# Moving the depthwise convolution of a Mamba block from VectorE to TensorE, and two of GpSimd's B x products per batch element to VectorE

## The chip, the cores and the metric

One core of one Trainium2 chip runs the whole program in one launch. The metric is the device time of the launch in microseconds. The engines are called by the profile's names: PE (TensorE), DVE (VectorE), ACT (ScalarE), POOL (GpSimd) and SP (SyncE, which only issues DMAs here).

## The reference, cut to what matters

```python
x = L0_attn_x                                   # 8 x 512 x 256, float32
x = x + layernorm(mamba(layernorm(x)))
x = x + layernorm(moe(layernorm(x)))            # 8 experts, top 1, and a shared one

def mamba(x):                                   # D_INNER 512, D_STATE 16, D_CONV 4
    h = (layernorm(x) * norm_w + norm_b) @ in_proj_w.T
    hp = pad(h, 3 rows in front)
    h = silu(sum(hp[:, k:k + L] * conv_w[:, k] for k in range(4)))
    dt_in, B, C = split(h @ x_proj_w.T, [1, 16, 16])
    dt = softplus(dt_in @ dt_proj_w.T + dt_proj_b)
    for t in range(L):                          # for each channel and each of 16 states n
        state = exp(A * dt[t]) * state + B[t] * h[t]
        y[t] = sum over n of state * C[t] + D * h[t]
    return silu(y) @ out_proj_w.T + x
```

The change concerns the sum over the four taps (`conv_w`) and the product `B[t] * h[t]`. Both exist once per batch element, and there are 8 batch elements of 512 time steps.

## The kernel before, in words

Channels lie on partitions: the 512 inner channels are four chunks `c` of 128, and a chunk's 512 time steps lie along the free dimension. One batch element is one iteration `i` of the outer loop. Inside it a step number `q` runs from 0 to 31: `q = 16 h + n` is state `n` for the two chunks of half `h`, so every instruction of a step works on 128x1024 values.

A step is a pipeline over four engines:

- ACT makes the decay `exp(A dt)` in PSUM, two activations per step (`decays`, L702). There are two decay buffers, so the decay of step q+2 waits for the scan of step q.
- `bx = B x` has a ring of four buffers. For even q POOL makes it (`inject`, L484), out of rows of B that a DMA has spread over all partitions (`bbc`). For odd q DVE makes it (`inject`, L1040), out of a PSUM bank `psB` that PE fills with a broadcast row (`spread_b`, L1403). `psB` is one bank, so the next broadcast waits for the last DVE product.
- DVE runs the recurrence with one scan instruction per step (`scan`, L1052), on a ring of eight state buffers.
- POOL multiplies the state by C (`weigh`, L495), and PE adds it up in PSUM (`total`, L1411, three steps behind).

All engines work through a program order that is written out by hand. In step q of iteration i each engine does its part of the scan of batch element i, then `front(i + 1, q)`, the projections of the next batch element, then `back(i - 1, q)`, the output projection and norms of the one before. Every engine takes its instructions in this order and waits on semaphores.

The convolution belongs to `front`. For chunk c, at the even step 2c+2, PE multiplies by `in_proj_w` into the PSUM bank `psF` (L1330), and ACT copies it to `acc` times the last tap (L613). At the odd step 2c+3 DVE adds the three shifted taps out of `psF` with three `scalar_tensor_tensor` (L998). PE's next in-projection waits for that, since `psF` is one bank. At step 10 ACT loads the table for silu and makes `xh` (L619), silu of y of the batch element before (L669), and loads the exp table again. At 11 PE makes `dt_in` (L1337), at 14 the B and C rows (L1343), which ACT copies (`prow_kept`). PE's output projection of the batch element before follows at 15 and 17 (L1373), and DVE adds its result (L1021) at 16 and 18. At 20 POOL subtracts for softplus (L500), at 22 DVE adds the residual (L1028), and at 23 and 24 DVE takes a minimum (L1012).

In the last iteration (batch element 7) there is no `front`. In the first there is no `back`. After the last batch element comes the mixture of experts, which the change does not touch.

```python
                if q in (2, 4, 6, 8):                       # ACT, front
                    act.wait_ge(inproj_ready, C * f + c + 1)
                    nc.scalar.activation(acc[:, c], psF[:], ACT.Identity, scale=cw[:, c, TAPS - 1:TAPS])
                if q in (3, 5, 7, 9):                       # DVE, front
                    for m in range(1, TAPS):
                        last = nc.vector.scalar_tensor_tensor(out=acc[:, c, m:L], in0=psF[:, 0:L - m], ...)
```

## Time and profile before

| | us |
|---|---|
| median of three runs | 1540.49 |
| lowest and highest run | 1537.66, 1542.84 |
| the profiled execution | 1531.43 |
| its span, first to last instruction | 1529.5 |
| busy in the span: PE, DVE, ACT, POOL | 1191.8, 1042.3, 802.7, 1022.1 |
| mean granted TensorE clock | 0.903 of full speed |

The profile is one execution. The eight iterations over the batch elements lie between about 45 and 1017 us of the span, and the experts behind them. Times of rows are microseconds from the span's start. An engine's idle time before a row is given with what ended it.

### The profile page before, as it was taken

What the parts mean: (1) busy time and instruction counts of PE and PEld (TensorE: products, weight loads), DVE (VectorE), ACT (ScalarE), POOL (GpSimd) and SP (SyncE); (2) the same over time, 40 slices, a digit from 0 to 9 for tenths busy, and PEclk for the clock granted to TensorE, in tenths of its full rate; (3) what the DMA queues carried; (4) which work ended last, traced back from release to release, by engine and by line L of the source; (5) the groups of instructions that cost most, each with busy time, mean ns of one, the idle gap of its engine ahead of it and who ended that gap; (6) DMA issues with size and microseconds to landing.
All of it is one profiled execution on the core that took longest, in us unless ns stands there. A gap on an engine that the chain in (4) does not pass through costs nothing. (4 is left out here: it accounts for less than half of the span.)

```text
span 1529.5 us, 15586 instructions
## 1 busy us (share of the span) xinstructions
PE 1191.8 (78%) x4766; PEld 525.4 (34%) x4767; DVE 1042.3 (68%) x1051; ACT 802.7 (52%) x1386; POOL 1022.1 (67%) x476
## 2 busy tenths in 40 slices
PE   5775867878878867787788786665999989999940
PEld 2321213323323223232232221223466656566520
DVE  4698998998998978998999998853211123233237
ACT  6665667768758657677677655353111111111137
POOL 0599999999999999999999999950470000000025
PEclk9896999999989889899898898877999999999975
DMA  2802302401311220240230240024941021111135
GB/s 60 313 0 70 125 0 71 147 19 57 127 53 57 90 91 2 97 138 2 96 125 2 69 152 1 14 96 157 343 157 38 0 86 43 46 41 42 44 110 178
DMA packets 77953, 128.46 MB, mean 84 GB/s; under 512 B 7616, under 2 KB 56384, under 8 KB 73792
## 3 DMA queue, kind: packets, MB, share of 16 engines
q1 hardware_dynamic: 67120, 108.93, 21.0%
q10 hardware_dynamic: 7696, 10.36, 1.9%
q0 software_dynamic: 3072, 8.39, 1.7%
q8 instruction: 30, 0.49, 0.1%
q14 instruction: 35, 0.29, 0.1%
HBM read 95.94 MB, written 31.72 MB: 83 GB/s over the span
## 5 line engine op out<-in xcount | busy, mean ns | idle before, releaser
L495 POOL TENSOR_TENSOR state<-state,cbc 128x1024 f32<-128x1024 f32 x256 | 611.6, 2410 | 11.5 <-DVE state L1052 11.4
L1052 DVE TENSOR_TENSOR_SCAN state<-psX,bx 128x1024 f32<-128x1024 f32 x256 | 577.9, 2278 | 44.4 <-ACT psX L702 19.6
L702 ACT ACTIVATE psX<-dt,aneg 128x511 f32<-128x511 f32 x512 | 330.7, 679 | 222.4 <-DVE state L1052 220.7
L484 POOL TENSOR_TENSOR bx<-xh,bbc 128x1024 f32<-128x1024 f32 x128 | 309.3, 2417 | 63.4 <-DMA bbc<-bc_rows 42.8
L1411 PE MATMUL psY<-state,ident 64*64 64x512 f32 x2048 | 302.5, 684 | 59.9 <-POOL state L495 59.9
L561 POOL DMA_INDIRECT fy<-slot_out,slot x32 | 33.2, 1037 | 339.8 <-DMA slot_out<-yo 330.4
L1403 PE MATMUL bank<-prow,ident 128*128 128x512 f32 x256 | 151.8, 677 | 105.0 <-DVE bx L1040 104.9
L1040 DVE TENSOR_TENSOR bx<-xh,bank 128x1024 f32<-128x1024 f32 x128 | 153.0, 1195 | 0.0
L1411 PEld LDWEIGHTS psY<-state,ident 64*64 64x64 f32 x2048 | 66.1, 144 | 249.3 <-issue 131.0
L1201 DVE TENSOR_TENSOR actN<-sg,psX 128x512 f32<-128x512 f32 x39 | 26.8, 688 | 141.1 <-ACT sg L901 141.1
L1403 PEld LDWEIGHTS bank<-prow,ident 128*128 128x128 f32 x256 | 43.1, 199 | 191.6 <-DVE bx L1040 148.9
L1154 DVE TENSOR_TENSOR actS<-sg,psX 128x512 f32<-128x512 f32 x32 | 21.9, 686 | 124.6 <-ACT sg L864 124.6
L901 ACT ACTIVATE sg<-psX 128x512 f32<-128x512 f32 x39 | 23.3, 597 | 157.5 <-PE psX L1515 157.5
L1515 PE MATMUL psX<-wg,xsT 128*128 x156 | 78.0, 623 | 0.7 <-DVE xsT L1195 0.6
L1515 PE MATMUL psX<-wu,xsT 128*128 x156 | 73.3, 592 | 0.0
L1330 PE MATMUL bank<-lt,win 128*128 128x512 f32 x112 | 59.2, 653 | 14.2 <-DVE acc L998 12.8
L1373 PE MATMUL bank<-wout,yv 128*128 128x256 f32 x256 | 62.4, 399 | 8.9 <-ACT yv L669 7.9
L864 ACT ACTIVATE sg<-psX 128x512 f32<-128x512 f32 x32 | 19.1, 597 | 92.5 <-PE psX L1462 92.5
L998 DVE SCALAR_TENSOR_TENSOR acc<-bank,cw,acc 128x511 f32<-128x511 f32 (+2 forms) x84 | 62.2, 741 | 3.0 <-ACT acc L613 1.0
L1462 PE MATMUL psX<-xg,shg 128*128 128x512 f32 x128 | 62.1, 608 | 1.7 <-DVE actS L1154 1.7
L1462 PE MATMUL psX<-xg,shu 128*128 128x512 f32 x128 | 60.5, 595 | 0.0
L1373 PEld LDWEIGHTS bank<-wout,yv 128*128 128x128 f32 x256 | 49.4, 198 | 28.8 <-issue 13.5
(183 smaller groups left out, 1554.8 us busy)
## 6 DMA issues: line engine op xcount, KB each, us to landing
cbc<-bc_rows SPq DMA_DIRECT2D x32, 1024.0 KB, 4.9
bbc<-bc_rows SPq DMA_DIRECT2D x16, 1024.0 KB, 6.2
slot_in<-ao SPq DMA_DIRECT2D x1, 4992.0 KB, 27.0
xsl<-slot_in SPq DMA_DIRECT2D x39, 128.0 KB, 2.2
slot_out<-yo ACTq DMA_DIRECT2D x39, 128.0 KB, 2.4
xin<-in_x SPq DMA_DIRECT2D x8, 512.0 KB, 5.4
xr<-in_x SPq DMA_DIRECT2D x8, 512.0 KB, 6.8
x_rows<-ao SPq DMA_DIRECT2D x8, 512.0 KB, 2.9
```

The lines of the kernel that those rows point to most:

```text
L484: nc.gpsimd.tensor_tensor(bx[q % RB][:], xh[par][:, h * CH:(h + 1) * CH], bbc[:, n // 2].unsqueeze(1).broadcast_to([P, CH, L]), ALU.mult). ...
L495: nc.gpsimd.tensor_tensor(w[:], w[:], cbc[:, n].unsqueeze(1).broadcast_to([P, CH, L]), ALU.mult).then_inc(weighted, 1)
L702: e = nc.scalar.activation(decay[q % RD][:, c, 1:L], dt[par][:, h * CH + c, 1:L], ACT.Exp, scale=aneg[:, h * CH + c, n:n + 1])
L998: last = nc.vector.scalar_tensor_tensor(out=acc[:, c, m:L], in0=psF[:, 0:L - m], scalar=cw[:, c, TAPS - 1 - m:TAPS - m], in1=acc[:, c, m:L ...
L1040: nc.vector.tensor_tensor(bx[q % RB][:], xh[par][:, h * CH:(h + 1) * CH], psB[:].unsqueeze(1).broadcast_to([P, CH, L]), ALU.mult).then_inc ...
L1052: nc.vector.tensor_tensor_scan(st[q % RS][:].rearrange("p c t -> p (c t)"), decay[q % RD].rearrange("p c t -> p (c t)"), bx[q % RB][:].rea ...
L1330: last = nc.tensor.matmul(psF[:], win[:, k, c * P:(c + 1) * P], hT[:, k], start=(k == 0), stop=(k == KC - 1))
L1373: last = nc.tensor.matmul(psF[:, (j % 2) * DIM:(j % 2 + 1) * DIM], yv[:, c, j * P:(j + 1) * P], wout[:, c], start=(c == 0), stop=(c == C - 1))
L1403: nc.tensor.matmul(psB[:], ident[:, n:n + 1].broadcast_to([P, P]), prow[par][:], start=True, stop=True).then_inc(b_bcast, 1)
L1411: done = nc.tensor.matmul(psY[o * HP:(o + 1) * HP, r], weights(half, c), src[half, c], start=first, stop=last_)
L1462: last = nc.tensor.matmul(bank, w[:, k, c * P:(c + 1) * P], xg[i][:, k], start=(k == 0), stop=(k == KC - 1))
L1515: last = nc.tensor.matmul(bank, xsT[i][:, k], w[:, bass.ds(ereg[i], 1), k].rearrange("p a n -> p (a n)"), start=(k == 0), stop=(k == KC - 1))
```

## The change

- In `front` of batch elements 1 to 7 ACT copies the in-projection from `psF` to `tmp` without a factor (step 2c+2). PE then writes the whole convolution of the chunk into `psF` as four accumulating matmuls with diagonal matrices of the taps (step 2c+3), each on the input shifted by m columns. ACT copies the result from `psF` to `acc` (step 2c+3). DVE's twelve tap instructions are gone. The first batch element keeps the old way.
- The 16 diagonal matrices (`dtap`) are made once, by four DVE instructions at the start.
- POOL makes `bx` for n = 0, 2, ... 12 only. Steps 14 and 30 go to DVE, with one more `spread_b` of PE for each. POOL has 14 and DVE 18 products per batch element. The B rows that the DMA spreads are seven and not eight.

```diff
+    POOL_N = [n for n in range(0, N - 2, 2)]
+    PN = len(POOL_N)
...
+    BY_POOL = [q % N in POOL_N for q in range(Q)]
...
@@ ACT front
                     act.wait_ge(inproj_ready, C * f + c + 1)
-                    nc.scalar.activation(acc[:, c], psF[:], ACT.Identity,
-                                         scale=cw[:, c, TAPS - 1:TAPS]).then_inc(tap_done, 1)
+                    nc.scalar.activation(tmp[:, c], psF[:], ACT.Identity).then_inc(tap_done, 1)
+                if q in (3, 5, 7, 9):
+                    c = q // 2 - 1
+                    act.wait_ge(conv_ready, C * (f - 1) + c + 1)
+                    nc.scalar.activation(acc[:, c], psF[:], ACT.Identity).then_inc(conv_done, 1)
@@ DVE front
-                if q in (3, 5, 7, 9):
-                    c = q // 2 - 1
-                    dve.wait_ge(tap_done, C * f + c + 1)
-                    for m in range(1, TAPS):
-                        last = nc.vector.scalar_tensor_tensor(
-                            out=acc[:, c, m:L], in0=psF[:, 0:L - m],
-                            scalar=cw[:, c, TAPS - 1 - m:TAPS - m], in1=acc[:, c, m:L],
-                            op0=ALU.mult, op1=ALU.add)
...
@@ DVE iteration
                         scan(i, q)
-                        if q % 2 == 0:
+                        if q + 1 < Q and not BY_POOL[q + 1]:
                             inject(i, par, q + 1)
@@ DVE first_front
+                for c in range(C):
+                    last = nc.vector.tensor_tensor(dtap[:, c], ident[:].unsqueeze(1).broadcast_to([P, TAPS, P]),
+                                                   cw[:, c].unsqueeze(2).broadcast_to([P, TAPS, P]), ALU.mult)
+                last.then_inc(taps_made, 1)
@@ PE front
+                if q in (3, 5, 7, 9):
+                    c = q // 2 - 1
+                    pe.wait_ge(taps_made, 1)
+                    pe.wait_ge(tap_done, C * f + c + 1)
+                    for m in range(TAPS):
+                        last = nc.tensor.matmul(psF[:, m:L], dtap[:, c, TAPS - 1 - m], tmp[:, c, 0:L - m],
+                                                start=(m == 0), stop=(m == TAPS - 1))
+                    last.then_inc(conv_ready, 1)
@@ PE iteration
-                    if q % 2 == 1:
+                    if not BY_POOL[(q + 2) % Q]:
                         if q + 2 < Q:
@@ POOL iteration
-                    if q % 2 == 0:
+                    if BY_POOL[(q + RB) % Q]:
                         if q + RB < Q:
                             inject(i, par, q + RB)
```

PE in iteration 1, steps 4 to 6 before (`bank0` is `psB`, `bank1` is `psF`, `L1403` the broadcast of B, `L1411` the total of one step, `L1330` the in-projection):

```order
L1330 MATMUL bank1<-lt,win 128x512 [waits conv_done]
L1330 MATMUL bank1<-lt,win 128x512
L1403 MATMUL bank0<-prow1,ident 128x512 [waits dve_bx]
L1411 MATMUL psY<-state2,ident 64x512 [waits weighted]
L1411 MATMUL psY<-state2,ident 64x512 x3
L1411 MATMUL psY<-state3,ident 64x512 [waits weighted]
L1411 MATMUL psY<-state3,ident 64x512 x3
L1330 MATMUL bank1<-lt,win 128x512 [waits conv_done]
```

The same place now (L1333 is the in-projection, L1414 the broadcast, L1422 the total):

```order
L1333 MATMUL bank1<-lt,win 128x512 [waits conv_done]
L1333 MATMUL bank1<-lt,win 128x512
L1414 MATMUL bank0<-prow1,ident 128x512 [waits dve_bx]
L1422 MATMUL psY<-state2,ident 64x512 [waits weighted]
L1422 MATMUL psY<-state2,ident 64x512 x3
L1341 MATMUL bank1<-tmp,dtap 128x512 [waits tap_done,taps_made]
L1341 MATMUL bank1<-tmp,dtap 128x511
L1341 MATMUL bank1<-tmp,dtap 128x510
L1341 MATMUL bank1<-tmp,dtap 128x509
L1422 MATMUL psY<-state3,ident 64x512 [waits weighted]
L1422 MATMUL psY<-state3,ident 64x512 x3
L1333 MATMUL bank1<-lt,win 128x512 [waits conv_done]
```

The four tap matmuls stand between the totals of two steps and ahead of the next in-projection, and they wait for ACT.

ACT in iteration 1, steps 4 to 6 now (`L713` is a decay, `L621` the copy out of the in-projection, `L625` the copy out of the convolution, `L585` to `L591` the norm factors of `back`):

```order
L713 ACTIVATE psX<-dt1,aneg 128x511 [waits scanned]
L713 ACTIVATE psX<-dt1,aneg 128x511
L621 ACTIVATE tmp<-bank1 128x512 [waits inproj_ready]
L713 ACTIVATE psX<-dt1,aneg 128x511 [waits scanned]
L713 ACTIVATE psX<-dt1,aneg 128x511
L625 ACTIVATE acc<-bank1 128x512 [waits conv_ready]
L585 ACTIVATE lnv0<-mv0,epsc 128x4 [waits mv_ready0]
L586 ACTIVATE nmr0<-mv0 128x4
L588 ACTIVATE rstd0<-lnv0 128x4 [waits rs_ready0]
L591 ACTIVATE nmr0<-nmr0,rstd0 128x1 [waits rs_ready0]
L591 ACTIVATE nmr0<-nmr0,rstd0 128x1 x3
L713 ACTIVATE psX<-dt1,aneg 128x511 [waits scanned,rs_ready0]
```

`L625` is new. It stands between the decays of two steps, and ahead of the norm factors and of every decay behind it.

DVE at the end of iteration 0 now, steps 28 to 31 and the scan of step 0 of iteration 1 (`L1051` is a scan, `L1039` a B x product; steps 12 to 15 read the same with other numbers):

```order
L1051 SCALAR_TENSOR_TENSOR state4<-psX,bx0 128x1024 [waits summed,decay_ready,pool_bx]
L1039 TENSOR_TENSOR bx1<-xh0,bank0 128x1024 [waits b_bcast]
L1051 SCALAR_TENSOR_TENSOR state5<-psX,bx1 128x1024 [waits summed,decay_ready,dve_bx]
L1039 TENSOR_TENSOR bx2<-xh0,bank0 128x1024 [waits b_bcast]
L1051 SCALAR_TENSOR_TENSOR state6<-psX,bx2 128x1024 [waits summed,decay_ready,dve_bx]
L1039 TENSOR_TENSOR bx3<-xh0,bank0 128x1024 [waits b_bcast]
L1051 SCALAR_TENSOR_TENSOR state7<-psX,bx3 128x1024 [waits summed,decay_ready,dve_bx]
L1051 SCALAR_TENSOR_TENSOR state0<-psX,bx0 128x1024 [waits summed,decay_ready,pool_bx]
```

Before, `bx2` of this place came from POOL and its scan waited for `pool_bx`. Now three DVE products follow each other through the one bank `psB`.

## Rows read from the trace of the kernel before

**Rows 1.** The page's costliest groups: count | busy, mean ns | idle before, releaser.

```profile
L495 POOL TENSOR_TENSOR state<-state,cbc 128x1024 f32<-128x1024 f32 x256 | 611.6, 2410 | 11.5 <-DVE state L1052 11.4
L484 POOL TENSOR_TENSOR bx<-xh,bbc 128x1024 f32<-128x1024 f32 x128 | 309.3, 2417 | 63.4 <-DMA bbc<-bc_rows 42.8
```

**Rows 2.** POOL's timeline, iteration 2: start us, us, instruction [idle before <-releaser].

```profile
305.74 4.70 POOL L495 TENSOR_TENSOR state<-state,cbc 128x1024 f32<-128x1024 f32 x2
310.35 2.40 POOL L484 TENSOR_TENSOR bx<-xh,bbc 128x1024 f32<-128x1024 f32 x1
312.67 4.71 POOL L495 TENSOR_TENSOR state<-state,cbc 128x1024 f32<-128x1024 f32 x2
...
371.55 2.35 POOL L495 TENSOR_TENSOR state<-state,cbc 128x1024 f32<-128x1024 f32 x1 [0.94 <-DVE state L1052]
...
378.48 4.53 POOL L500 TENSOR_TENSOR lt<-lt,dt 128x2048 f32<-128x2048 f32 x1
```

**Rows 3.** POOL's timeline, the same instruction in iteration 3.

```profile
497.73 4.52 POOL L500 TENSOR_TENSOR lt<-lt,dt 128x2048 f32<-128x2048 f32 x1
```

**Rows 4.** DVE's timeline, iterations 1 (first row) and 2.

```profile
290.39 2.29 DVE L1052 TENSOR_TENSOR_SCAN state<-psX,bx 128x1024 f32<-128x1024 f32 x1 [0.81 <-ACT psX L702]
...
304.10 1.20 DVE L1040 TENSOR_TENSOR bx<-xh,bank 128x1024 f32<-128x1024 f32 x1
...
307.71 2.29 DVE L998 SCALAR_TENSOR_TENSOR acc<-bank,cw,acc 128x511 f32<-128x511 f32 x3
...
312.12 1.20 DVE L1040 TENSOR_TENSOR bx<-xh,bank 128x1024 f32<-128x1024 f32 x1
...
345.57 4.47 DVE L1052 TENSOR_TENSOR_SCAN state<-psX,bx 128x1024 f32<-128x1024 f32 x2 [0.69 <-ACT psX L702]
...
360.00 0.69 DVE L1021 TENSOR_TENSOR ao<-bank,ao 128x512 f32<-128x512 f32 x1 [3.08 <-PE bank L1373]
...
380.78 3.31 DVE L1028 TENSOR_TENSOR ao<-ao,xr 128x1024 f32<-128x1024 f32 x1 [0.24 <-ACT ao L590]
```

**Rows 5.** ACT's timeline, iteration 2.

```profile
305.46 1.06 ACT L692 ACTIVATE yv<-psY 128x512 f32<-128x512 f32 x2
306.58 0.69 ACT L613 ACTIVATE acc<-bank,cw 128x512 f32<-128x512 f32 x1
...
317.44 0.28 ACT L577 ACTIVATE lnv<-mv,epsc 128x4 f32<-128x4 f32 x1
...
318.09 0.85 ACT L583 ACTIVATE nmr<-nmr,rstd 128x1 f32<-128x1 f32 x4
...
325.44 2.06 ACT L590 ACTIVATE ao<-xr,nmr,rstd 128x256 f32<-128x256 f32 x4
...
336.61 1.30 ACT L702 ACTIVATE psX<-dt,aneg 128x511 f32<-128x511 f32 x2 [3.11 <-DVE state L1052]
...
344.24 2.52 ACT L702 ACTIVATE psX<-dt,aneg 128x511 f32<-128x511 f32 x4
```

**Rows 6.** PE's timeline, iteration 2.

```profile
304.56 1.98 PE L1330 MATMUL bank<-lt,win 128*128 128x512 f32 x4
306.38 1.02 PE L1403 MATMUL bank<-prow,ident 128*128 128x512 f32 x2
...
339.48 1.99 PE L1411 MATMUL psY<-state,ident 64*64 64x512 f32 x8
341.40 3.71 PE L1337 MATMUL bank<-xh,xp 128*128 128x512 f32 x8
345.04 1.09 PE L1411 MATMUL psY<-state,ident 64*64 64x512 f32 x8
...
350.74 3.70 PE L1343 MATMUL bank<-xh,w_bc 128*128 128x512 f32 x8 [1.68 <-ACT acc L624]
```

**Rows 7.** DVE's timeline, the last iteration.

```profile
959.05 0.69 DVE L1021 TENSOR_TENSOR ao<-bank,ao 128x512 f32<-128x512 f32 x1 [5.24 <-PE bank L1373]
...
979.64 8.76 DVE L1028 TENSOR_TENSOR ao<-ao,xr 128x1024 f32<-128x1024 f32 x1 [0.20 <-ACT ao L590]
```

29 lines of the change are left out of this document (15 added, 14 removed).

## The prediction

> **What bounds the kernel now.** I read the page first. POOL's two instructions of the state loop are busy for 611.6 and 309.3 us and wait little for anyone: 11.5 us, and 63.4 less 42.8 at the start, so 32 us over all eight iterations [rows 1]. That makes POOL look like the bound. In its timeline two steps take 312.67 - 305.74 = 6.93 us for three instructions, so 2.31 us each [rows 2]. One iteration takes 497.73 - 378.48 = 119.25 us [rows 2, 3]. POOL's own work in it is 48 x 2.31 + 4.5 = 115.4 us, and about 3 us more by which DVE slows it. It waits for DVE once, 0.94 us [rows 2].
>
> Then I read DVE in the same iteration. It never waits for POOL directly. In the steps with the convolution two steps take 312.12 - 304.10 = 8.02 us [rows 4], more than POOL's 6.93, and POOL lives on the lead that DVE has. So two loops are nearly equally long: POOL's, and a chain that goes through DVE, ACT and PE. The 0.94 us say that the second is the longer one. Its waits tell where it leaves DVE: scan 13 waits 0.69 us for a decay, the add at step 16 waits 3.08 us for PE, scan 30 waits 0.81 us for a decay [rows 4]. A kernel with this shape gets faster only where both loops get shorter. So each part of the change is priced on the chain.
>
> **Part 1, the convolution, steps 2 to 13.** It removes 12 tap instructions per iteration from DVE, 2.2 us for each chunk of three [rows 4], so 8.8 us. What replaces them lies in one line, since `psF` is one bank: in-projection (PE), copy (ACT), four taps (PE), copy (ACT), next in-projection. Prices: four 512-column matmuls in float32 take 3.7 us (two groups, 3.71 and 3.70) and the in-projection 1.8 us until the next group begins [rows 6]. A broadcast or a total takes 1.0 us of PE [rows 6]. A copy without a factor takes 0.6 us, a little over half of the 1.06 us of two [rows 5].
>
> The first chunk: scan 2 ends at 304.1 [rows 4], ACT has kept y at 306.5 [rows 5], PE then does the D total and the total of step 0 (0.1 + 0.9 + 1.0), and the taps start at 308.5. Chunk to chunk: 3.7 taps, 0.6 copy, 0.1, 1.8 in-projection, 1.0 broadcast, 1.0 total = 8.2 us. So two chunks later it is 324.9. For the last chunk ACT is the longer way, because behind its wait stand the norm apply of 2.06 us and a decay pair of 1.25 us [rows 5]: 3.7 + 0.6 + 2.1 + 1.25 + 0.6 + 0.1 = 8.3, and the last taps start at 333.2. The norm factors (317.44 to 318.94, [rows 5]) fit beside PE's work. The taps end at 336.9 and the copy at 337.6. Then comes the decay of step 12, which ACT began at 336.61 before, and behind it the two tables, both silus and the decay of step 13: scan 13 began 8.96 us after that point [rows 4, 5]. So it begins at 346.5 now, and began at 345.57 before: **+0.9 us**. DVE's 8.8 us are gained as DVE time and lost as waits for decays that stand behind ACT's copies.
>
> At this place a rule of the Trainium skill speaks otherwise. The rows show 3.7 us for four matmuls [rows 6]. The page "TensorE: Matmul & The Clock Gate", section "Back-to-back issue gap", gives 216 ns for one of 512 columns at full clock; by that, an estimate, four taps would be 0.9 us and this part would gain some 10 us an iteration. The trace decides for 3.7.
>
> **Part 2, POOL's two products go to DVE.** POOL sheds 2 x 2.31 = 4.6 us an iteration [rows 2], and DVE takes 2 x 1.2 us [rows 4]. On the chain POOL's part counts for nothing here: it will wait longer for scans instead. Of DVE's part, product 14 stands in front of the 3.08 us wait at step 16 [rows 4], which would cover it. But through `psB` it holds PE: the broadcast for step 15 now waits until product 14 is done, 346.5 + 2.2 + 1.2 = 349.9, and behind it on PE stand two totals and the B and C rows (L1343). They start at 349.9 + 1.0 + 0.9 + 1.0 = 352.8, and started at 350.74, after 1.68 us of idle [rows 6]. The output projection and the add wait for them. So the add comes 2.1 us late, 0.9 of it from part 1: **+1.2 us**. If PE finds one total already done, it is 0.2; if not even the idle is used, 2.4. Product 30 stands before scan 30, which waits 0.81 us for ACT anyway [rows 4]. Between 1.2 - 0.81 = 0.4 and 1.2 us stay, and I take **+0.6 us**, near the low end, since the wait stands right behind the product. The broadcast that it needs lies in PE time between waits, and it delays ACT's copies about as much.
>
> **The rest.** The four `dtap` instructions run while DVE waits for ACT before the first scan, and cost nothing; without this cover they cost at most 4 x 0.7 us. The seventh row of B less to load is off every wait. The factor moves out of ACT's copy for 0.1 us, counted above.
>
> **The sum.** Iterations 1 to 6: 6 x (0.9 + 1.2 + 0.6) = 16.2 us. Iteration 0 has no `back`, and from step 10 POOL is behind there with every instruction, so only the last term counts: +0.6. The last iteration has no convolution, and PE and with it DVE wait 5.24 us for POOL's pace before the add [rows 7]. There POOL's products of step 30 before and step 14 count, -4.7, and DVE's product 30 in the tail +1.2: -3.5. Together 16.2 + 0.6 - 3.5 = 13.3, so **+13 us**. On the profiled execution (1531.4) that is 1544.4. The median shown is 9.1 us above that execution, and I put the same 13 us on it: **1553.5 us**. If an iteration costs as little as 0.5 us or as much as 4.5, the sum is 0 to +24 us, so 1541 to 1565.
>
> **The rivals.**
>
> *POOL is the bound, faster.* If the chain has more slack than I count, each of the 16 products removed is worth its 2.31 us [rows 2]: -37 us, 1503. For it: POOL's idle of 32 us in all [rows 1]. Against it: the 0.94 us and the 8.2 us per chunk above, which is more than POOL's 6.93 and than DVE's 8.02. It decides if the chunk-to-chunk line is under 7 us. Chance 0.12, of which 0.02 for taps at the page's price.
>
> *The terms cancel.* The waits of 0.69, 3.08 and 0.81 us [rows 4] swallow all of product 14 and 30, and PE runs a chunk in 7.9. Then iterations 1 to 6 stand still and only the last gains: -2 us, 1538, give or take 6. Chance 0.18.
>
> *PE's clock, slower still.* After an idle stretch the same total took 1.99 us where it takes 1.09 [rows 6], so there the array went at 1.2 and not 2.4 GHz. If one of the four tap groups per iteration meets this, it costs 3.4 us more, 6 x 3.4 = 20: 1573. Against it: PE is nearly gapless in these steps now. Chance 0.10.
>
> *The residual add locked out, slower still.* DVE's add of two SBUF tensors took 3.31 us in iteration 2 and 8.76 us in the last one, for the same 1024 columns [rows 4, 7]; POOL worked through beside it. If POOL's new phase makes the long form the rule, six iterations cost 5.4 us each: +33, 1586. Chance 0.08. The Trainium skill's page "SBUF — State Buffer" (ports and contention) says that such a DVE instruction waits until POOL's one in progress is finished. By that rule the most would be one POOL instruction, and this rival would cost nothing; the 8.76 us here are longer than three of them.
>
> **How the numbers follow.** The forecast has 0.52. A measurement of this kernel tells about 0.3%, 4.6 us, from no change. Faster: POOL as the bound 0.12 and a third of the cancelled case 0.06, together 0.18. Same: 0.10 of the cancelled case and 0.08 of the forecast's low end, 0.18. Slower: the rest, 0.64. The range goes from 1533, the low end of the cancelled case, to 1570, just short of the clock case. It leaves out the POOL case (0.12) and most of the last two.
>
> **What would show it.** Right: scans 6, 8, 10 and 13 wait for decays (DVE state <- ACT psX grows by 5 to 9 us an iteration), POOL waits for scans 5 us or more an iteration, ACT waits for the convolution's matmuls, and the chunk-to-chunk distance is 8.2 us. Scan 13 comes 42.4 us after the end of scan 2, and L500 repeats every 122 us. Wrong: L500 repeats in under 119 us, POOL's idle stays near 32 us, or the tap group takes clearly less than 3.7 us.

## The result and the profile after

The changed kernel takes 1579.4 us (median of 4 runs, 1575.2 to 1580.9) where the kernel before takes 1540.0: the ratio is 1.0254, with a 95% interval of 1.0230 to 1.0278. That is +39 us; the forecast was +13. The profiled execution has a span of 1577.7 us.

| | before | after |
| --- | --- | --- |
| span, us | 1529.5 | 1577.7 |
| up to scan 3 of iteration 0 | 66.0 | 66.8 |
| iteration 0, scan 3 to the next scan 3 | 120.8 | 124.5 |
| iterations 1 to 6 | 722.0 | 758.9 |
| last iteration, scan 3 to scan 31 | 103.7 | 100.4 |
| behind the last scan | 517.0 | 527.1 |
| POOL busy, us | 1022.1 | 985.5 |
| DVE busy, us | 1042.3 | 1007.5 |
| PE busy, us | 1191.8 | 1303.7 |

The part behind the last scan is not touched by the change: the profiles of all kernels have 515 to 527 us there (first experiment). The loop lost 38 us, and the six middle iterations 37 of them.

The page's groups of the changed kernel, which answer to [rows 1] (busy, mean ns | idle before, releaser):

```profile
L503 POOL TENSOR_TENSOR state<-state,cbc 128x1024 f32<-128x1024 f32 x256 | 611.6, 2407 | 74.4 <-DVE state L1051 74.3
L1051 DVE TENSOR_TENSOR_SCAN state<-psX,bx 128x1024 f32<-128x1024 f32 x256 | 578.1, 2279 | 118.1 <-ACT psX L713 86.8
```

POOL now waits 74.3 us for scans in this line (before 11.4). The scans wait 86.8 us for decays (before 19.6). POOL has been relieved and stands idle; the chain grew.

DVE's timeline, iteration 2, which answers to [rows 4]: start, us, instruction [idle before <-releaser].

```profile
314.87 1.19 DVE L1039 TENSOR_TENSOR bx<-xh,bank 128x1024 f32<-128x1024 f32 x1
...
335.10 2.29 DVE L1051 TENSOR_TENSOR_SCAN state<-psX,bx 128x1024 f32<-128x1024 f32 x1 [4.08 <-ACT psX L713]
...
343.87 2.29 DVE L1051 TENSOR_TENSOR_SCAN state<-psX,bx 128x1024 f32<-128x1024 f32 x1 [2.89 <-ACT psX L713]
...
357.98 2.29 DVE L1051 TENSOR_TENSOR_SCAN state<-psX,bx 128x1024 f32<-128x1024 f32 x1 [3.51 <-ACT psX L713]
...
375.29 0.69 DVE L1020 TENSOR_TENSOR ao<-bank,ao 128x512 f32<-128x512 f32 x1 [3.45 <-PE bank L1384]
...
396.07 3.31 DVE L1027 TENSOR_TENSOR ao<-ao,xr 128x1024 f32<-128x1024 f32 x1 [0.24 <-ACT ao L598]
...
423.35 2.29 DVE L1051 TENSOR_TENSOR_SCAN state<-psX,bx 128x1024 f32<-128x1024 f32 x1 [2.07 <-ACT psX L713]
...
441.16 1.19 DVE L1039 TENSOR_TENSOR bx<-xh,bank 128x1024 f32<-128x1024 f32 x1
```

ACT's timeline, the last copy of the convolution and the tables' load behind it:

```profile
348.53 0.60 ACT L625 ACTIVATE acc<-bank 128x512 f32<-128x512 f32 x1 [2.89 <-PE bank L1341]
349.02 1.29 ACT L713 ACTIVATE psX<-dt,aneg 128x511 f32<-128x511 f32 x2
350.33 1.28 ACT L630 ACT_TABLE_LOAD   x1
```

Scan 2 ends at 314.87 and again at 441.16, so an iteration lasts 126.3 us (before 119.6). The waits for decays in front of scans 8, 10 and 13 are the ones that were named. Scan 13 begins 43.1 us after the end of scan 2 (before 41.5, forecast 42.4). The residual add (L1027) kept its length of 3.31 us.

PE's timeline of the same iteration, which answers to [rows 6], with a chunk of the convolution, product 14's broadcast, and the first dt sums:

```profile
319.51 3.69 PE L1341 MATMUL bank<-tmp,dtap 128*128 128x512 f32 x8
323.13 1.09 PE L1422 MATMUL psY<-state,ident 64*64 64x512 f32 x8
324.15 1.98 PE L1333 MATMUL bank<-lt,win 128*128 128x512 f32 x4
325.97 1.02 PE L1414 MATMUL bank<-prow,ident 128*128 128x512 f32 x2
326.92 1.09 PE L1422 MATMUL psY<-state,ident 64*64 64x512 f32 x8
327.94 3.69 PE L1341 MATMUL bank<-tmp,dtap 128*128 128x512 f32 x8
...
361.44 1.12 PE L1414 MATMUL bank<-prow,ident 128*128 128x512 f32 x2 [2.27 <-DVE bx L1039]
362.49 3.38 PE L1422 MATMUL psY<-state,ident 64*64 64x512 f32 x16
365.80 3.92 PE L1354 MATMUL bank<-xh,w_bc 128*128 128x512 f32 x8
...
404.80 2.07 PE L1368 MATMUL bank<-acc,ident 128*128 128x512 f32 x2 [1.17 <-ACT acc L660]
406.66 1.91 PE L1369 MATMUL bank<-tmp,ident 128*128 128x512 f32 x2
408.37 1.92 PE L1370 MATMUL bank<-lt,minus 128*128 128x512 f32 x2
```

Three things stand here. From tap group to tap group it is 327.94 - 319.51 = 8.43 us, without a gap: PE itself sets the pace. Behind the broadcast that waited for product 14, two totals take 3.38 us, where the same sixteen matmuls took 1.93 to 1.95 us elsewhere. And the three dt sums of the first chunk all run at twice their usual 1.02 us. The kernel before had its third one back at full clock:

```profile
389.52 2.07 PE L1357 MATMUL bank<-acc,ident 128*128 128x512 f32 x2 [1.18 <-ACT acc L649]
391.38 1.66 PE L1358 MATMUL bank<-tmp,ident 128*128 128x512 f32 x2
392.88 1.02 PE L1359 MATMUL bank<-lt,minus 128*128 128x512 f32 x2
```

The granted clock says the same. PE in four stretches of the changed kernel: length, busy (x), granted clock, DMA share, GB/s.

```profile
359.20:361.40 2.20, 0.00 (x0) 1.00 0.00 0
361.40:362.80 1.40, 1.36 (x6) 1.00 0.00 0
363.00:366.00 3.00, 3.00 (x17) 0.50 0.00 0
404.80:410.50 5.70, 5.70 (x7) 0.50 0.01 1
```

0.50 is the level of 1.2 GHz. In the wait for product 14 itself the clock was still full, and so it was for the first 1.4 us of work behind it. It fell at 362.9, in the middle of the totals. Ahead of the dt sums PE had waited 3.6 and 1.2 us.

**One table for all kernels.** Since every kernel keeps the same loop, I read the starts of all 256 scans off DVE's timeline and took the distances from scan to scan (where the timeline merges two scans into one row, the border is put in its middle, which can move a start by 0.03 us). They are means over iterations 1, 2, 4, 5 and 6 (in iteration 3, scan 31 to the next scan takes 4 to 8 us more in every kernel). Each row is one profiled execution. The scans in no column take 53.6 to 54.0 us together in every kernel, so the columns hold all that moves.

| kernel | 3 to 13 | 13 to 14 | 16 to 17 | 22 to 23 | 28 to 29 | 29 to 30 | 31 to 0 | iteration |
| --- | --- | --- | --- | --- | --- | --- | --- | --- |
| before | 39.8 | 2.24 | 7.10 | 6.89 | 4.32 | 3.10 | 2.29 | 119.3 |
| after | 42.0 | 3.53 | 7.99 | 6.90 | 5.46 | 3.53 | 2.62 | 125.7 |
| before, second profile | 39.9 | 2.24 | 7.10 | 6.89 | 4.88 | 3.10 | 2.29 | 120.0 |
| after, second profile | 42.0 | 3.53 | 7.98 | 6.89 | 5.42 | 3.53 | 2.62 | 125.6 |
| convolution alone | 42.6 | 2.24 | 7.10 | 6.89 | 4.35 | 3.11 | 2.29 | 122.3 |
| split alone | 39.6 | 3.53 | 7.00 | 6.89 | 5.13 | 3.53 | 2.62 | 122.0 |
| after, 30 kept on POOL | 42.1 | 3.53 | 7.32 | 6.88 | 5.18 | 3.10 | 2.29 | 124.1 |
| after, 14 kept on POOL | 42.2 | 2.24 | 7.10 | 6.88 | 4.64 | 3.53 | 2.62 | 122.7 |
| after, DVE copies | 40.5 | 3.53 | 7.98 | 6.89 | 5.02 | 3.53 | 2.62 | 123.7 |
| DVE copies, old split | 41.1 | 2.24 | 7.06 | 6.82 | 4.89 | 3.10 | 2.29 | 121.1 |
| after, zeros before 15 | 42.0 | 3.53 | 7.61 | 6.88 | 4.74 | 3.53 | 2.62 | 124.5 |
| after, zeros before dt | 42.2 | 3.53 | 7.33 | 6.90 | 3.48 | 3.53 | 2.61 | 123.2 |
| after, both zeros | 42.0 | 3.53 | 7.63 | 6.91 | 3.48 | 3.53 | 2.61 | 123.3 |
| before, zeros before dt | 40.5 | 2.24 | 7.10 | 8.32 | 3.76 | 2.45 | 2.29 | 120.2 |
| before, zeros, pause | 40.5 | 2.24 | 7.10 | 6.96 | 3.48 | 2.25 | 2.29 | 118.6 |
| bf16 taps | 31.7 | 3.92 | 7.33 | 11.16 | 4.79 | 3.53 | 2.62 | 118.8 |
| bf16, old split | 32.5 | 2.24 | 7.55 | 16.77 | 4.39 | 3.11 | 2.29 | 122.7 |
| bf16, old split, pause | 33.8 | 2.24 | 7.57 | 10.06 | 4.53 | 3.10 | 2.29 | 117.5 |
| bf16, zeros | 32.4 | 4.13 | 7.32 | 8.34 | 3.63 | 3.53 | 2.61 | 115.7 |
| bf16, zeros, pause | 32.4 | 3.70 | 7.33 | 7.12 | 3.47 | 3.53 | 2.62 | 114.1 |

The second row less the first is +6.3 us: +2.2 in the convolution's steps, +2.2 from product 14 to the step-16 add, +1.9 around product 30. The two profiles of the changed kernel agree. Those of the kernel before differ by 0.56 us from scan 28 to 29, so against its second profile the last term is only +1.3: differences of half a microsecond in that column are not told apart here.

### The profile page after: what moved, and what is told of

Read it like the earlier page. It is cut to its first block and busy times, and to the rows that moved or that the text cites. A ratio compares the mean times of both kernels' runs of the same rounds, so it can differ in the third digit from the quotient of the medians.

```text
span 1577.7 us, 16102 instructions
## 1 busy us (share of the span) xinstructions
PE 1303.7 (83%) x5022; PEld 574.2 (36%) x5023; DVE 1007.5 (64%) x987; ACT 810.3 (51%) x1414; POOL 985.5 (62%) x460
## 5 line engine op out<-in xcount | busy, mean ns | idle before, releaser
L503 POOL TENSOR_TENSOR state<-state,cbc 128x1024 f32<-128x1024 f32 x256 | 611.6, 2407 | 74.4 <-DVE state L1051 74.3
L1051 DVE TENSOR_TENSOR_SCAN state<-psX,bx 128x1024 f32<-128x1024 f32 x256 | 578.1, 2279 | 118.1 <-ACT psX L713 86.8
L713 ACT ACTIVATE psX<-dt,aneg 128x511 f32<-128x511 f32 x512 | 330.2, 679 | 116.3 <-DVE state L1051 114.4
L1422 PE MATMUL psY<-state,ident 64*64 64x512 f32 x2048 | 296.4, 666 | 37.6 <-POOL state L503 37.5
L492 POOL TENSOR_TENSOR bx<-xh,bbc 128x1024 f32<-128x1024 f32 x112 | 271.1, 2421 | 74.1 <-DMA bbc<-bc_rows 43.2
L1414 PE MATMUL bank<-prow,ident 128*128 128x512 f32 x288 | 169.4, 672 | 71.1 <-DVE bx L1039 71.1
L1039 DVE TENSOR_TENSOR bx<-xh,bank 128x1024 f32<-128x1024 f32 x144 | 172.1, 1195 | 7.0 <-PE bank L1414 7.0
L1422 PEld LDWEIGHTS psY<-state,ident 64*64 64x64 f32 x2048 | 63.5, 141 | 225.5 <-issue 142.4
L1414 PEld LDWEIGHTS bank<-prow,ident 128*128 128x128 f32 x288 | 53.3, 209 | 163.4 <-DVE bx L1039 108.5
L1341 PE MATMUL bank<-tmp,dtap 128*128 128x512 f32 (+1 forms) x224 | 103.3, 604 | 0.0
L1157 DVE TENSOR_TENSOR actS<-sg,psX 128x512 f32<-128x512 f32 x32 | 21.9, 686 | 124.5 <-ACT sg L875 107.2
L625 ACT ACTIVATE acc<-bank 128x512 f32<-128x512 f32 x28 | 16.7, 597 | 96.6 <-PE bank L1341 96.6
L1341 PEld LDWEIGHTS bank<-tmp,dtap 128*128 128x128 f32 x224 | 40.2, 189 | 62.8 <-issue 62.8
```

Source lines behind the costliest of these rows:

```text
L492: nc.gpsimd.tensor_tensor(bx[q % RB][:], xh[par][:, h * CH:(h + 1) * CH], bbc[:, n // 2].unsqueeze(1).broadcast_to([P, CH, L]), ALU.mult). ...
L503: nc.gpsimd.tensor_tensor(w[:], w[:], cbc[:, n].unsqueeze(1).broadcast_to([P, CH, L]), ALU.mult).then_inc(weighted, 1)
L713: e = nc.scalar.activation(decay[q % RD][:, c, 1:L], dt[par][:, h * CH + c, 1:L], ACT.Exp, scale=aneg[:, h * CH + c, n:n + 1])
L1039: nc.vector.tensor_tensor(bx[q % RB][:], xh[par][:, h * CH:(h + 1) * CH], psB[:].unsqueeze(1).broadcast_to([P, CH, L]), ALU.mult).then_inc ...
L1051: nc.vector.tensor_tensor_scan(st[q % RS][:].rearrange("p c t -> p (c t)"), decay[q % RD].rearrange("p c t -> p (c t)"), bx[q % RB][:].rea ...
L1341: last = nc.tensor.matmul(psF[:, m:L], dtap[:, c, TAPS - 1 - m], tmp[:, c, 0:L - m], start=(m == 0), stop=(m == TAPS - 1))
```

## The experiments

Ratios are to the kernel before, timed beside each group of runs; in brackets the 95% interval. That kernel took 1541 us beside the first four and 1531 to 1533 beside the others, so ratios are compared and not times.

### Two controls

The kernel before, profiled once more, no edit.

> The kernel before once more, for a second profile beside the one shown (span 1529.5, of which 517.0 behind the last scan, against 523 to 527 in the five other profiles). Theory: the part behind the last scan was short by chance in the profile shown, so this one has 521 to 527 there and a span near 1539, with the scans of iterations 1 to 6 in 720 to 727. Rival: it is 517 again, and moving the convolution or the products costs 6 to 10 us in the expert part too.

Measured: 1536.8 us in one run, span 1534.8, of which 517.9 behind the last scan; iterations 1 to 6 take 725.0. The theory fell: 517 is no chance of one profile. The rival falls too, with the next run: the part differs between groups of runs and not between kernels. The four kernels of the first group, with or without the change's parts, have 523 to 527 there, all later ones 515 to 521. That accounts for the 8 us between 1541 and 1532.

The changed kernel once more, no edit, beside a kernel before of 1530.6:

> The changed kernel itself once more, since the runs with zero matmuls stand beside a kernel before of 1531 to 1533, and the changed kernel beside one of 1540. Theory (what differs is the part behind the last scan, 517 instead of 525 us, the same for both kernels): 1.025 to the kernel before again, within 0.002, so 1569 to 1573 where that has 1532; the part behind the last scan 516 to 520. Rival (the loss itself depends on the chip): under 1.020, and the zero matmuls brought less than the ratios say.

Measured: 1570.3 us, 1.0259 (1.0242 to 1.0276), 519.2 us behind the last scan, 125.6 us an iteration. The loss is the same, and the ratios of all groups can be compared.

### The convolution alone, the split alone

```diff
-    POOL_N = [n for n in range(0, N - 2, 2)]
+    POOL_N = [n for n in range(0, N, 2)]
```

> The changed kernel, but POOL keeps all sixteen products (states 0, 2, ..., 14), so only the convolution is moved. Theory (the loss has three places, and the convolution's own is +1.6 us an iteration, from the end of scan 2 to scan 13; the products' are +2.9 and +2.2): about 1549 us, 1545 to 1556. Rival 1 (the conv on PE carries the whole loss, since it fills PE and makes everything behind it late): 1570 to 1580. Rival 2 (with the old split the chain has slack for it again): 1540, within 4.

Measured: 1556.7 us, 1.0110 (1.0089 to 1.0131), +15.6 us, just above the theory's range. The only column that moves is the first, 39.8 to 42.6: 2.8 us where the theory had 1.6 from iteration 2 alone.

The other half keeps the change's split and puts the three `scalar_tensor_tensor` taps back on DVE, with the factor in ACT's copy; PE's taps are gone.

> The kernel before, with the change's split alone: products 14 and 30 by DVE, the convolution on DVE as before. Theory (product 14 costs the step-16 add 2.9 us and product 30 costs 2.2 us before the next iteration, through PE's broadcasts): 6 x 5 = 30, so 1565 to 1575. Rival 1 (these terms arise only behind a convolution on PE, which fills PE and makes it late): under 1555. Rival 2 (POOL is the bound and is relieved of 37 us): under 1530.

Measured: 1549.3 us, 1.0049 (1.0032 to 1.0066), +8.2 us. The table shows product 14 at its 1.29 us and no dip in scan 16 to 17 (6.85 to 7.23 in every iteration), and 0.8 + 0.4 + 0.3 us around product 30. So rival 1 was the nearer: alone, the split costs far less than the 30 us of my theory. The two halves bring 15.6 + 8.2 = 23.8 of the 39.4 us. The rest, 15.6 us, arises only together, and the profiles show only part of it: 3 us in iteration 0 (+0.5 and +0.2 us alone, +3.7 together) and, in iterations 1 to 6, +36.9 us against 16.8 + 17.6 alone (+33.9 against 13.8 + 14.6 by the second profile of the kernel before), so 2.5 to 5.5 us, where the clock's dips from scan 16 to 17 come in. What makes up the remainder is open.

### One product each

```diff
-    BY_POOL = [q % N in POOL_N for q in range(Q)]
+    BY_POOL = [q % 2 == 0 and q != 14 for q in range(Q)]
```

> The changed kernel, but POOL keeps product 30, so only product 14 goes to DVE. Theory (2.9 us an iteration belong to product 14 before the step-16 add, 2.2 to product 30): the changed kernel less 6 x 2.2 = 13 less nothing else: 1566, 1562 to 1571. Rival (what one product costs is swallowed by waits and only both together hurt): 1550 to 1556. Rival (POOL's load decides and the relief of product 30 was worth its 2.3 us): slower than the changed kernel, 1585 or more.

Measured: 1569.4 us, 1.0188 (1.0161 to 1.0216), in the theory's range. The table has product 14 at 13 to 14 with its full 1.29 us. The dip behind its broadcast came in two iterations of six (scan 16 to 17: 8.50 and 8.87 us), against four in the changed kernel. Scan 28 to 29 is 0.9 us longer than before (0.3 against the second profile) although product 30 is POOL's here.

With `q != 30` in place of 14:

> The changed kernel, but POOL keeps product 14, so only product 30 goes to DVE. Convolution alone stood at 1.011 and with product 14 at 1.0188. Theory (product 30 costs 0.8 us at scans 29 and 31 through the broadcast, and up to 1.1 through the clock): 4 to 11 above the convolution alone, ratio 1.014 to 1.018; scan 16 to scan 17 stays 7.1 in every iteration. Rival (product 30 is swallowed by the wait of scan 30, as product 14 is the one that breaks the clock): 1.011 within 0.002.

Measured: 1.0125 (1.0104 to 1.0147), inside the rival's 1.011 within 0.002 and below the theory's 1.014. By time it is not told apart from the convolution alone (1.0089 to 1.0131). Product 30 costs 0.3 + 0.4 + 0.3 = 1.0 us an iteration over the convolution alone by the table (+0.5 in its sum, since scans 3 to 13 are 0.4 shorter), and scan 16 to 17 stays at 7.0 to 7.2 everywhere. Of the 1.9 us that I had found around product 30, then, 1.0 are its own. The other 0.9 seem to come with product 14 (5.18 for it against 4.35 for the convolution alone), but that is hardly more than the 0.56 us between two profiles of the kernel before, so this share is not shown.

### Who copies the convolved chunk

```diff
 ACT, step 3, 5, 7, 9:
-                    act.wait_ge(conv_ready, C * (f - 1) + c + 1)
-                    nc.scalar.activation(acc[:, c], psF[:], ACT.Identity).then_inc(conv_done, 1)
 DVE, step 4, 6, 8, 10:
+                    dve.wait_ge(conv_ready, C * (f - 1) + c + 1)
+                    nc.vector.tensor_copy(acc[:, c], psF[:]).then_inc(conv_done, 1)
```

> The changed kernel, but the copy of the convolved chunk from psF to acc is done by DVE, behind scans 4, 6, 8 and 10, so ACT no longer stands before PE's taps. Theory A (the line through psF, 8.43 us a chunk, sets scan 13, and who copies matters little): 1579 within 5; taps start 8.3 to 9 us apart. Theory B (the decays that stand in ACT behind its wait for the taps are what makes the scans late): the scans' waits for decays shrink from 12 to under 6 us an iteration, scan 13 comes 1.5 to 3 us earlier after the end of scan 2, and the time is 1560 to 1570.

Measured: 1563.4 us, 1.0142 (1.0125 to 1.0159). Theory B: the scans wait 16.9 us for decays in the whole run instead of 86.8, and scans 3 to 13 take 40.5 instead of 42.0 us. But the waits did not vanish, they changed place: DVE now waits for the taps itself (scan 6 to 7 and 8 to 9 are 6.2 us), and the tap groups still start 8.43 us apart. What was won is what ACT lost by standing before PE's taps.

With the old split as well:

> The changed kernel with DVE's copies of the convolved chunks and POOL's old eight products. DVE's copies took 16 us from the changed kernel, the old split 23. Theory (the two act at different scans, 5 to 13 against 13 to 17 and 28 to 31, and add up but for POOL's loop): ratio 1.000 to 1.005. Rival (both shorten the same line): ratio 1.008 to 1.012.

Measured: 1.0076 (1.0048 to 1.0104), at the rival's edge: the two do not add up, and with float32 taps no placing of copies and products reached the kernel before.

### PE's clock

Matmuls that add zero to the open sums in `psY` fill PE's waits. `before_spread`, `before_total` and `after_total` are the places in PE's step.

```diff
+            def keep_clock(par, n):
+                for _ in range(n):
+                    for r in range(2):
+                        for k in range(2):
+                            nc.tensor.matmul(psY[k * HP:(k + 1) * HP, r], ident[r * HP:(r + 1) * HP, (1 - r) * HP:(2 - r) * HP],
+                                             prow[par][r * HP:(r + 1) * HP, :], start=False, stop=False)
 zeros before 15:  before_spread {13: 2}
 zeros before dt:  before_spread {21: 2, 23: 1}, before_total {24: 3}, after_total {24: 1}
```

> The changed kernel, with eight more matmuls by a zero block of ident into psY (they add zero) on PE just before the broadcast for step 15, where PE waits 2.27 us for product 14. In four of six iterations the totals behind that wait took 3.38 us, and scan 16 to scan 17 took 8.5 instead of 6.85. Theory (the granted clock falls in this wait and makes the add 1.65 us late): the distance from scan 16 to scan 17 is 6.85 to 7.2 in all six, 4 x 1.65 = 6.6 less: 1573, 1569 to 1576. Rival (the totals are long because two of them queue, not because of the clock): no gain or a loss of up to 4, 1579 to 1583.

Measured: 1558.9 us, 1.0161 (1.0130 to 1.0192). That is 14 us off, more than the theory gave, and at another place: scan 16 to 17 still takes 7.9 to 8.2 us in four of the six iterations, but scan 28 to 29 fell from 5.46 to 4.74. (The four runs lie at 1554 and at 1563 us, and the profile is of one at 1563, so the table's row shows less than the median's gain.) The zeros moved the dips; they did not remove them.

> The changed kernel, with such zero matmuls in PE's waits at steps 21 (8), 23 (4) and 24 (12 before and 4 after the total of step 21), ahead of the dt sums. In the changed kernel the dt sums of the first chunk run at the lower clock to their end (2.07, 1.92, 1.91 us), before they had recovered for the third (1.02). Theory (the clock's late recovery is 0.9 us of the 1.2 us by which scan 29 comes later): the distance from scan 28 to scan 29 falls from 5.4 to 4.2 or less, 6 x 1.2 = 7, and up to 3 us more an iteration where even the first sums run at full clock: 1556 to 1573. Rival (scan 29 is late through product 30 and the broadcast): 1577 to 1583.

Measured: 1556.5 us, 1.0155 (1.0138 to 1.0172). PE's timeline of it:

```profile
399.88 1.13 PE L1368 MATMUL bank<-acc,ident 128*128 128x512 f32 x2 [0.81 <-ACT acc L660]
400.85 1.02 PE L1369 MATMUL bank<-tmp,ident 128*128 128x512 f32 x2
401.70 1.02 PE L1370 MATMUL bank<-lt,minus 128*128 128x512 f32 x2
```

The first chunk's sums are at full clock, 2.8 us from the first start to the last end where the changed kernel has 5.5, and scan 28 to 29 takes 3.48 us, 2.0 less. Product 30 is still DVE's here, so most of this stretch was the clock. Scan 16 to 17, where no zeros stand, fell as well, from 7.99 to 7.33: one long distance in six iterations where the changed kernel has four.

> The changed kernel (float32 taps) with both sets of zero matmuls, ahead of the broadcast for step 15 and ahead of the dt sums; alone they brought 14 and 15 us. Theory (the clock's share is 1.65 us in four of six iterations at the first place and 1.2 to 2 at the second; part of each one's gain was the other's place met by chance): 18 to 24 less than the changed kernel, ratio 1.010 to 1.014, and what is left is the convolution's 2.2 and product 14's 1.2 us. Rival (fully additive): 1.006. Rival (the two overlap fully): 1.015.

Measured: 1555.7 us, 1.0172 (1.0150 to 1.0193), the rival of full overlap. Both together bring no more than either alone. The table fits that: the zeros before dt had by themselves already taken most of the dips at scan 16 to 17, and each set alone shortened the other's place too. Why filling PE at one place changes when the clock falls at another was not tried.

The same zeros in the kernel before:

> The kernel before with the same zero matmuls ahead of the dt sums. There the first two sums took 2.07 and 1.81 us against 1.02 at full clock. Theory (the clock costs the kernel before the same way, and these sums lie on the chain): 1.5 to 2 us an iteration less in the distance from scan 28 to scan 29, six times: 1528 to 1534. Rival (POOL's 115.4 us of work an iteration and its loop hold it): 1538 to 1542. Rival (the zero matmuls delay the totals): 1543 to 1548.

Measured: 0.9999 (0.9989 to 1.0009). Scans 28 to 30 are 1.2 us shorter and nothing is gained. The table shows the takers: scans 3 to 13 with +0.7, and scan 22 to 23, 8.32 instead of 6.89, all of it in iteration 6, where the residual add took 10.46 us. That is the lock that the prediction had as a rival.

### Short taps

```diff
+        dtap = sb("dtap", [P, C, TAPS, P], BF16, where=A)
+        tap_in = sb("tap_in", [P, C, L], BF16, where=A)
-                    nc.scalar.activation(tmp[:, c], psF[:], ACT.Identity).then_inc(tap_done, 1)
+                    nc.scalar.activation(tap_in[:, c], psF[:], ACT.Identity).then_inc(tap_done, 1)
```

> The changed kernel, with the diagonal matrices and the copied in-projection rounded to bf16 (the convolution alone is rounded; sums stay float32). In float32 four taps take 3.7 us; the estimate for bf16 is half the passes or less, 0.9 to 1.9 us. Theory (the line in-projection, copy, taps, copy through psF sets scan 13): chunk to chunk falls from 8.43 to 5.6 to 6.6 us, the waits of scans 8, 10 and 13 vanish, scans 3 to 13 take 35 to 37 us instead of 41.95, and POOL's loop takes over; the two products by DVE then pay: 1545 to 1555 on a chip where the changed kernel has 1579 (ratio 1.003 to 1.01). Rival (the decays behind scan 12 hold it, not PE): under 1 us an iteration less, ratio 1.02 to 1.025.

Measured: 1515.5 us, 0.9892 (0.9873 to 0.9911), further than the theory. Four bf16 taps take 1.03 us:

```profile
307.09 1.03 PE L1342 MATMUL bank<-tap_in,dtap 128*128 128x512 bf16 x4
```

Scans 3 to 13 take 31.7 us, 8.1 less than before: DVE's freed 8.8 us arrive almost whole. So the line through `psF` was the bound in these steps, and the price of four float32 matmuls is what made it long. The profile is of a run of 1521.9 us, 6 above the median; in it four of the six residual adds of iterations 1 to 6 took 10.3 to 10.6 us, which is why scan 22 to 23 stands at 11.16. The same kernel with POOL's old split:

> The bf16 taps with POOL's old eight products. Theory (with short taps POOL's loop of 115.4 us of work plus waits is the bound, and products 14 and 30 on DVE relieve it): slower than or equal to the bf16 taps with the change's split, ratio 0.995 to 1.01 to the kernel before. Rival (products 14 and 30 still cost 3.6 us an iteration at the broadcasts, whatever the taps cost): faster than the same with the change's split by 8 to 20, ratio 0.98 to 0.995.

Measured: 1542.3 us, 1.0076 (1.0059 to 1.0093), 27 us slower. That is in the theory's range, but not for its reason: here the products on DVE pay, and the table has it in one column, scan 22 to 23, with 16.77 us against 11.16 and 6.9 in the changed kernel. All six adds are long.

> The bf16 taps with the change's split and the zero matmuls ahead of the dt sums. Theory (the two gains are at different places and add): 10 to 15 less than the bf16 taps alone. Rival (with short taps POOL is the bound): equal to them within 4.

Measured: 1503.7 us, 0.9848 (0.9804 to 0.9893), 12 us less than without the zeros. The size is the theory's, the reason only in part. Of the 3.1 us an iteration by which the profiles differ, scan 28 to 29 has 1.2 and scan 22 to 23 has 2.8, less 0.7 lost in scans 3 to 13: most of the gain is that two adds are long in this profile and not four. So this run doesn't show that the clock's gain adds to that of the short taps.

### The lock

In the old split with bf16 taps, DVE's add and POOL's work beside it, iteration 5, DVE first:

```profile
744.18 13.74 DVE L1028 TENSOR_TENSOR ao<-ao,xr 128x1024 f32<-128x1024 f32 x1 [0.24 <-ACT ao L599]
```

```profile
743.06 2.41 POOL L504 TENSOR_TENSOR state<-state,cbc 128x1024 f32<-128x1024 f32 x1
745.37 4.57 POOL L509 TENSOR_TENSOR lt<-lt,dt 128x2048 f32<-128x2048 f32 x1
749.83 2.41 POOL L504 TENSOR_TENSOR state<-state,cbc 128x1024 f32<-128x1024 f32 x1
752.13 2.40 POOL L493 TENSOR_TENSOR bx<-xh,bbc 128x1024 f32<-128x1024 f32 x1
754.44 2.40 POOL L504 TENSOR_TENSOR state<-state,cbc 128x1024 f32<-128x1024 f32 x1
```

POOL's last instruction ends at 756.8, because it has run out of scans (the next one stands behind the add on DVE); the add ends at 757.9. It needs 1.2 us of work and was done 1.1 us after POOL's end, having let five POOL instructions pass, the one in progress and four more. One wait more on POOL tests this:

```diff
+                    if q == 21 and not (isinstance(i, int) and i == 0):
+                        pool.wait_ge(x1_ready, i)
                     weigh(i, q)
```

> The bf16 taps with POOL's old split, and one wait more on POOL: before it weighs step 21 it waits for DVE's residual add of step 22. Without it that add of two SBUF tensors takes 13.6 us for 1.2 us of work, and ends where POOL next runs out of work. Theory (DVE is locked out until POOL pauses, however many instructions POOL has in a row): the add falls to under 6 us, scan 22 to scan 23 from 16.8 to under 10, and the time by 25 to 45 us: ratio 0.980 to 0.992 against 1.0076. Rival (the page's rule, DVE waits for the one POOL instruction in progress, and the long form has another cause such as the 2048-element subtraction): the add keeps 8 us or more and POOL's pause costs 1 to 2 us an iteration: ratio 1.007 to 1.02.

Measured: 1514.9 us, 0.9896 (0.9878 to 0.9913), 27 us less for a wait that was added. DVE's and POOL's timelines now:

```profile
727.84 6.65 DVE L1030 TENSOR_TENSOR ao<-ao,xr 128x1024 f32<-128x1024 f32 x1 [0.24 <-ACT ao L601]
```

```profile
728.91 4.50 POOL L509 TENSOR_TENSOR lt<-lt,dt 128x2048 f32<-128x2048 f32 x1
734.65 2.34 POOL L504 TENSOR_TENSOR state<-state,cbc 128x1024 f32<-128x1024 f32 x1 [1.24 <-DVE ao L1030]
```

The add went in as soon as POOL paused, 1.1 us before its own end, and POOL lost 1.24 us. So the lock is shown: a pause of POOL ends it, also one that was made for it. The ratio is in the theory's range, its two distances are not: the adds took 5.5 to 6.9 us and not under 6, since each still waits for POOL's instruction in progress and in most iterations for the subtraction behind it, and scan 22 to 23 takes 10.06 us. The old split with the pause (1514.9 us) is as fast as the change's without it (1515.5). That is no comparison of the splits, for the latter keeps four long adds; the change's split with the pause and without zeros was not run.

> The bf16 taps with the change's split, the zero matmuls ahead of the dt sums, and POOL's wait for the residual add. Scan 22 to scan 23 is 8.3 us there on average, 1.4 over the undisturbed 6.9. Theory (only the long forms of the add are cut): 5 to 10 less than without the wait, ratio 0.978 to 0.983. Rival (POOL, now without slack, pays for its pause on the chain): 0.985 to 0.992.

Measured: 1485.0 us, 0.9696 (0.9676 to 0.9716), 46 us faster than the kernel before, the best version found. It is 19 us less than without the wait, where the theory had 5 to 10: the profiles have 14.4 us of it in iterations 1 to 6 and 6.2 in the last one, whose add fell from 8.53 to 3.15 us and which the theory left out. It has the change's split, its convolution on PE with input and taps rounded to bf16, the zeros and the pause.

> The kernel before (convolution on DVE, its own split), with the zero matmuls ahead of the dt sums and POOL's wait for the residual add. The zero matmuls alone brought nothing there: scan 29 came 0.6 to 1 us earlier an iteration, but the residual add took the long form once (10.5 us in iteration 6). Theory (that lock ate the gain): ratio 0.990 to 0.996. Rival (POOL's 115.4 us of work and its loop hold the kernel before, and the pause costs POOL): 1.000 to 1.006.

Measured: 0.9958 (0.9942 to 0.9975), at the theory's slow edge. With zeros and pause in the kernel before, all in float32, the 10.46 us add is gone, the last iteration's add takes 3.14 instead of 8.76 us, and 6.5 us are gained. That is the fastest version here that rounds nothing.

## Why the prediction was wrong

The direction and the places were right. The sizes were not, and one cost, PE's clock behind the longer waits, stood in no term of the sum. Loop terms, forecast and measured (a second figure is by the second profile of the kernel before):

| term | forecast | measured |
| --- | --- | --- |
| scans 2 to 13, per iteration | +0.9 | +2.2 |
| product 14 to the add, per iteration | +1.2 | +2.2 |
| product 30, per iteration | +0.6 | +1.9, +1.3 |
| iteration 0 | +0.6 | +3.7, +2.9 |
| last iteration | -3.5 | -3.3 |

**"Chunk to chunk: 3.7 taps, 0.6 copy, 0.1, 1.8 in-projection, 1.0 broadcast, 1.0 total = 8.2."** Every price was right and the sum was of the wrong line. PE takes its instructions in order, and between taps and in-projection stands a total of 1.02 us. It covers the copy of 0.6 but is itself in the line: 3.62 + 1.02 + 1.82 + 0.95 + 1.02 = 8.43, by the starts shown. Over three chunks that is some 0.6 us (the last had 8.3 in the forecast), and the first tap group starts 4.64 instead of 4.4 us after scan 2. From the last copy to scan 13 the forecast's 8.9 us came true (349.1 to 357.98). In iteration 2 this makes +1.6 instead of +0.9; over the five iterations it is +2.2, because the kernel before is faster there in the others. That the convolution costs at all is settled by the bf16 taps.

**"They start at 349.9 + 1.0 + 0.9 + 1.0 = 352.8."** This is the step that failed in part 2. It prices two totals behind a wait at full clock. The product's own +1.3 came as forecast, and with the split alone so did the add. But beside the convolution, in four of six iterations PE's clock fell 1.4 us after the 2.27 us for which the broadcast had waited, and the totals took 3.38 us instead of 1.95. The second place is the dt sums, whose third group also stayed at 1.2 GHz. I had the clock as a rival and put it in the wrong spot: on a tap group, where PE is gapless, with "PE is nearly gapless in these steps" as the argument against. That argument was right for the taps (all 28 groups take 3.69 us) and said nothing of PE's waits at the broadcast for step 15 and ahead of the dt sums, which the change lengthens or shifts. The rival's 20 us compares with 14 and 15 us that either set of zeros brought back. That agreement is luck, since no tap group met the lower clock. The 14 and 15 us are what filling brings, and part of them may be clock that the kernel before lacks too, so they are not the clock's exact share of the +39.

**"The broadcast that it needs lies in PE time between waits, and it delays ACT's copies about as much."** Product 30 itself costs 1.0 us instead of 0.6. Its broadcast for step 31 waits for the product, and behind it on PE stand a total and the transposes (L1398), for which ACT waits 1.45 us (before 0.32). The decays of the next scans stand behind that. What else lies in the +1.3 to +1.9 is not settled. The step looked at the wait in front of scan 30 and not at the queue behind the broadcast.

**"Iteration 0 has no back, and from step 10 POOL is behind there with every instruction, so only the last term counts."** It is false for the two together. In all four kernels scan 24 of this iteration starts 14.7 us after the start of POOL's subtraction for softplus: ACT waits for that, and DVE's minimum of step 23 behind ACT is locked out until POOL runs dry (last section). So iteration 0 is as long as POOL needs to reach the subtraction, which comes 70.6 us after scan 3 in the kernel before, 71.6 with the convolution alone, 70.6 with the split alone and 74.1 with both. With both, POOL still waited 2.54 us for a scan 48.6 us after scan 3, long past step 10; in the kernel before its last wait was at 37 us.

The last iteration was right to 0.2 us. "What would show it" came true for the places of the waits and for POOL (10.7 us for scans in its line L503 in iteration 2). It failed for the sizes: the scans' waits for decays grew by 11 us in that iteration (2.8 to 13.8) and not by 5 to 9, scan 13 came after 43.1 and not 42.4 us, chunk to chunk took 8.43 and not 8.2, and an iteration 126.3 and not 122 us.

**The rivals.** *POOL is the bound*: false for this kernel. With the taps at 1.03 us the chunk line is 5.8 us, under the 7 us from which I had said that it decides, and the two products are then worth 27 us. But the table has that gain where the residual add stands, so it comes through the lock; that POOL's own time was the bound is not shown. The Trainium skill's 216 ns for one matmul of 512 columns ("TensorE: Matmul & The Clock Gate", section "Back-to-back issue gap") agrees with the bf16 taps of this case, which start 0.216 us apart, and not with the float32 ones, which start 0.86 us apart. *The terms cancel*: of the waits of 0.69, 3.08 and 0.81 us only the last swallowed something: scan 29 to 30 grew by 0.43 us for a product of 1.2. *The residual add locked out*: it did not happen in iterations 1 to 6 of the changed kernel, whose adds begin at the same point of POOL's subtraction as before (last section); the last iteration's add took 10.06 us, where it was 8.76. In the faster versions it decides much of the time. The Trainium skill's page "SBUF — State Buffer" (section "SBUF: two separate sides") lets such an add wait for the one POOL instruction in progress; the 3.31 us of the changed kernel fit that, the 13.74 us beside five POOL instructions do not.

## What to carry to other kernels

When an engine works in order, price a line through it with every instruction that stands between, not only with those of the new work, and look at what stands behind each wait that a change lengthens: here a broadcast's wait held totals, transposes and, through them, the decays. Read PE's granted clock behind every wait that a change adds or moves, and fill such waits with harmless matmuls once before judging the change. Where an engine is said to be behind, follow it to its last wait with the whole change priced in, as two parts that each leave it behind may together catch it up. And an engine's idle time can be worth keeping, since another may need its pauses.

## What the hardware did that I had not expected

**A DVE instruction with two SBUF inputs can be held until POOL pauses.** Over the 17 profiles without the added wait there are 119 residual adds in the iterations. 89 took 3.0 to 3.4 us, and 30 took 8.5 to 13.8. Each long one ended some 1.1 us after POOL had run out of scans; POOL's next instruction came 2.28 us later, since it waits for the scan behind the add. How long POOL had run without a pause doesn't decide: adds 81, 123 and 128 us after its last one were short (3.4 us). Where the add begins in POOL's instruction separates them but for one: all 29 that began up to 2.12 us after its start were long, and of the 90 that began 2.18 us or more after it, which all met the subtraction of 2048 columns (4.5 us), 89 were short. The one exception is iteration 2 of the bf16 taps (2.25 us after the start, 10.31 us long). No experiment moved that point alone, so this is a pattern and not a shown cause.

It is not only that add. In iteration 0 of every kernel DVE's first minimum (L1012), which also reads two SBUF tensors, takes 8.2 to 8.3 us instead of 1.2; it begins 2.1 us after the start of a POOL instruction. Here it is in the kernel before, and POOL beside it, which runs dry at 150.3; the minimum ends at 151.4:

```profile
143.13 8.25 DVE L1012 SCALAR_TENSOR_TENSOR lt<-lt,dt 128x1024 f32<-128x1024 f32 x1 [6.85 <-ACT dt L647]
```

```profile
145.67 4.63 POOL L495 TENSOR_TENSOR state<-state,cbc 128x1024 f32<-128x1024 f32 x2
153.66 2.35 POOL L484 TENSOR_TENSOR bx<-xh,bbc 128x1024 f32<-128x1024 f32 x1 [3.36 <-DVE state L1052]
```

**A wait that was added gave 27 us** (1.0076 to 0.9896), by letting that add in.

**The granted clock's dips move.** Zero matmuls in a wait at step 13 shortened a stretch at steps 28 to 29 by 0.7 us and left four of six long distances at step 16, at 7.9 to 8.2 instead of 8.5 to 8.9 us. Two sets together brought no more than one. How the chip picks the moment was not tried.

**Four float32 matmuls of 512 columns take 3.69 us, four in bf16 1.03 us.** From start to start it is 0.86 against 0.216 us, a factor of 4.
